# Attention, mixture-of-experts block on one core: row maxima turned into rows by VectorE instead of TensorE and ScalarE

## The reference

```
x:[8, 512, 512] fp32
x = x + layernorm(attention(layernorm(x)))      # 16 heads of 32, latent K/V/Q (128), rotary part shared by the heads
    c_kv, c_q = x @ W_DKV + b, x @ W_DQ + b
    k = [c_kv @ W_UK + b | (x @ W_KR + b) * pe],  q = [c_q @ W_UQ + b | (x @ W_QR + b) * pe],  v = c_kv @ W_UV + b
    attn = softmax(q . k / sqrt(32));  out = (attn @ v) @ W_O + b
x = x + layernorm(moe(layernorm(x)))            # 16 experts, top 2 of 16 in 2 of 4 groups, plus a shared expert (1024)
```

## Time and profile before

| | us |
|---|---|
| median of 3 runs | 1569.3 (1569.14 to 1573.41) |
| span of the profiled execution | 1566.3 |
| median less that span (what lies around it, and the spread of executions) | 3.0 |
| PE busy | 1498.5 (96%), 7006 instructions |
| DVE busy | 974.3 (62%), 1841 instructions |
| ACT busy | 783.3 (50%), 1415 instructions |
| POOL busy | 803.9 (51%), 812 instructions |
| POOL busy from 60 to 900 us | 633.75 of 840 |
| DVE busy from 60 to 900 us | 573.16 of 840 |

### The profile page before, as it was taken

How to read it: one execution, slowest core, us unless ns; L and a number is a source line. 1 busy time by engine, 2 the same in 40 slices (tenths; PEclk the granted TensorE clock), 3 DMA queues, 4 the chain that set the end, 5 groups by cost and what they waited for, 6 DMA issues and landing times.

```text
span 1566.3 us, 21725 instructions
## 1 busy us (share of the span) xinstructions
PE 1498.5 (96%) x7006; PEld 1018.5 (65%) x7006; DVE 974.3 (62%) x1841; ACT 783.3 (50%) x1415; POOL 803.9 (51%) x812
## 2 busy tenths in 40 slices
PE   5699999999999999999998999999999999999998
PEld 3355666656656666566564578778666666668886
DVE  3657676767676767767667454862333333349988
ACT  3265567566565675665647455422222222275554
POOL 1076787787776977877859630003222222143341
PEclk9699999999999999999999999999999999999999
DMA  5878669589495795884956421536987777697773
GB/s 130 138 100 135 101 109 213 74 173 172 82 179 111 121 211 74 181 156 85 222 97 129 135 79 67 198 121 196 311 235 219 210 215 221 195 349 241 232 241 125
DMA packets 163926, 257.75 MB, mean 165 GB/s; under 512 B 20100, under 2 KB 70404, under 8 KB 161764
## 3 DMA queue, kind: packets, MB, share of 16 engines
q1 hardware_dynamic: 144584, 204.98, 58.0%
q0 software_dynamic: 12784, 41.82, 9.4%
q10 hardware_dynamic: 6448, 9.57, 1.8%
HBM read 103.74 MB, written 58.46 MB: 104 GB/s over the span
## 4 chain that ended last, share of the span: by engine, by line
PE 71%; DMA 10%; DVE 7%; POOL 4%; issue 3%; ACT 2%; SPq 2%; DVEq 0%; POOLq 0%; ACTq 0%
PE bank L113 12%; PE bank L724 9%; PE bank L792 8%; PE bank L815 8%; PE bank L646 6%; PE bank L632 6%; DMA a<-a 6%; PE bank L662 6%; PE bank L651 6%; PE bank L746 5%; POOL a L1637 2%; PE bank L671 2%; DMA f<-f 1%; SPq L1875 1%; PE bank L804 1%
## 5 line engine op out<-in xcount | busy, mean ns | idle before, releaser
L1637 POOL TENSOR_TENSOR a<-a 128x512 f32<-128x512 f32 x384 | 499.5, 1329 | 100.2 <-ACT a L1443 54.5
L1443 ACT ACTIVATE a<-bank 128x512 f32<-128x512 f32 x512 | 296.4, 597 | 258.4 <-PE bank L651 218.4
L925 DVE TENSOR_REDUCE a<-bank 128x1 f32<-128x512 f32 x512 | 321.3, 680 | 80.2 <-PE bank L632 79.7
L113 PE MATMUL bank<-a 128*128 128x512 f32 (+1 forms) x864 | 238.9, 398 | 2.7 <-DVE s L877 1.6
L646 PE MATMUL bank<-a 128*128 128x512 f32 x512 | 217.3, 424 | 5.0 <-ACT a L1443 4.9
L651 PE MATMUL bank<-a 68*128 68x512 f32 x512 | 203.8, 398 | 0.4 <-ACT a L1433 0.2
L632 PE MATMUL bank<-a 128*128 128x512 f32 x512 | 181.0, 425 | 22.7 <-DMA a<-a 17.8
L113 PEld LDWEIGHTS bank<-a 128*128 128x128 f32 (+1 forms) x864 | 158.9, 186 | 49.1 <-issue 6.7
L1701 POOL DMA_INDIRECT f<-h_scratch,f x79 | 75.4, 954 | 224.5 <-DMA f<-f 203.6
L746 PE MATMUL bank<-c 128*128 128x512 f32 x768 | 178.2, 391 | 4.2 <-DVE c L983 2.1
L724 PE MATMUL bank<-c 128*128 128x512 f32 x768 | 177.4, 390 | 1.3 <-ACT c L1484 1.3
(11 more groups left out here) (190 smaller groups left out, 1766.9 us busy)
## 6 DMA issues: line engine op xcount, KB each, us to landing
a<-a SPq DMA_DIRECT2D x272, 256.0 KB, 9.7
f<-f SPq DMA_DIRECT2D x316, 64.0 KB, 3.9
yp_scratch<-f SPq DMA_DIRECT2D x79, 256.0 KB, 3.4
a<-in_L_attn_x SPq DMA_DIRECT2D x15, 1024.0 KB, 11.7
x_scratch<-a SPq DMA_DIRECT2D x8, 1024.0 KB, 4.6
h_scratch<-a SPq DMA_DIRECT2D x8, 1024.0 KB, 13.3
hT_scratch<-s SPq DMA_DIRECT2D x8, 1024.0 KB, 9.8
c<-hT_scratch SPq DMA_DIRECT2D x8, 1024.0 KB, 7.0
```

The costliest lines, as they stand in the source:

```text
L113: t = e.matmul(out, a[n], b[n], start=n == 0 and m == 0, stop=n == len(ah) - 1 and m == 2)
L925: e.tensor_reduce(K.mx[:, i, j:j + 1], K.MX[n % 3][:], AX.X, ALU.max).then_inc(Z.max, 1)
L1443: e.activation(K.pt[:, n % NP, :], K.SC[n % 2][:], ACT.Exp, scale=SCALE).then_inc(Z.exp, 1)
L1637: e.tensor_tensor(K.acc[:, j, :], a, K.pt[:, n % NP, :], ALU.add).then_inc(Z.acc, 1)
```

## The change

`rows` leaves the lists of PE and ScalarE and joins the list of VectorE at the same place in the order. `K.mx` becomes [128, 4, 32], set to zero once by POOL, so that each block i of maxima fills the first 4 of 32 columns. One block transpose of VectorE (32x32 blocks) turns the 128x128 of `K.mx` into `K.mt`, in which partition 32q + j holds the maxima of head j for queries 32q to 32q+31 of each block. Four multiplies by -1, one for each q, take 4 partitions and 4x32 elements each and write them to their columns of `K.QR[64:68]`. The `scores` matmuls wait for the new semaphore `max_rows_set`.

```diff
-FILLS = ("turn", "proj", "half", "rows", "v", "total", "project", "turn2", "route", "fold", "bias")
+FILLS = ("turn", "proj", "half", "v", "total", "project", "turn2", "route", "fold", "bias")
-    K.mx = tile([P, 4, 4])
+    K.mx = tile([P, 4, HD])
+    K.mt = tile([P, 4, HD])
 # tensor_program
-    def rows(u):
-        bank = begin("rows", u)
-        w.wait_ge(Z.max, 16 * (u + 1))
-        for i in range(4):
-            t = e.transpose(bank[0:4, i * P:(i + 1) * P], K.mx[:, i, :], K.ident[:])
-        t.then_inc(*end("rows", u))
     def scores(u, i, j):
...
-        drained("rows", u)
+        w.wait_ge(Z.rows, u + 1)
 # vector_program
     def top(u, j, i):
         n = 16 * u + 4 * j + i
         w.wait_ge(Z.top, n + 1)
+        w.wait_ge(Z.set, 3)
         if u:
-            m = K.fill["rows", u - 1]
-            w.wait_ge(Z.full[m % 2], m // 2 + 1)
+            w.wait_ge(Z.mT, u)
...
+    def rows(u):
+        w.wait_ge(Z.max, 16 * (u + 1))
+        if u >= 2:
+            w.wait_ge(Z.score, 16 * (u - 1))
+        if u:
+            w.wait_ge(Z.rows, u)
+        e.transpose(K.mt.rearrange("p i r -> p (i r)"), K.mx.rearrange("p i r -> p (i r)")).then_inc(Z.mT, 1)
+        w.wait_ge(Z.mT, u + 1)
+        tiles = K.QR[64:68, u % 2, :].rearrange("p (i q r) -> p i q r", q=4, r=HD)
+        for q in range(4):
+            t = e.tensor_scalar(tiles[:, :, q, :], K.mt[HD * q:HD * q + 4, :, :], -1.0, None, ALU.mult)
+        t.then_inc(Z.rows, 1)
 # scalar_program
-    def rows(u):
-        b = u // NG
-        bank = begin("rows", u)
-        if u >= 2:
-            w.wait_ge(Z.score, 16 * (u - 1))
-        e.mul(K.QR[64:68, u % 2, :], bank[0:4, :], -1.0).then_inc(*end("rows", u))
 # gpsimd_program
+    e.memset(K.mx, 0.0).then_inc(Z.set, 1)
```

More of the change, by code:

```diff
@@ L382, in __init__ @@
         self.x1, self.hi = make("x1_done"), make("kq_high")
-        self.top, self.max = make("top_full"), make("max_done")
+        self.top, self.max, self.rows, self.mT = make("top_full"), make("max_done"), make("max_rows_set"), make("max_turned")
         self.score, self.exp, self.acc, self.pv = make("score_full"), make("exp_done"), make("acc_done"), make("pv_done")
@@ L755, in totals @@
         e.matmul(K.TR[0][:], K.tri, flat, start=True, stop=True).then_inc(Z.totals, 1)
-        w.wait_ge(Z.set, 3)
+        w.wait_ge(Z.set, 4)
         e.matmul(K.TR[1][:], K.onesf, flat, start=True, stop=True).then_inc(Z.totals, 1)
@@ L817, in e_down @@
         t.then_inc(Z.ed, 1)
-    stages = {"turn": turn, "proj": proj, "v": v, "half": half, "bias": bias, "top": top, "rows": rows, "scores": scores,
+    stages = {"turn": turn, "proj": proj, "v": v, "half": half, "bias": bias, "top": top, "scores": scores,
               "values": values, "total": total, "project": project, "turn2": turn2, "route": route, "fold": fold, "up": up,
@@ L1342, in finish @@
         e.tensor_tensor(K.x1[:, z, :], K.x1[:, z, :], K.sh[:, z, :], ALU.add).then_inc(Z.co, 1)
-    stages = {"stat": stat, "aggr": aggr, "sel": sel, "split w": split_w, "turn": turn, "low": low, "proj": proj, "half": half, "bias": bias, "top": top, "invert": invert,
+    stages = {"stat": stat, "aggr": aggr, "sel": sel, "split w": split_w, "turn": turn, "low": low, "proj": proj, "half": half, "bias": bias, "top": top, "rows": rows, "invert": invert,
               "project": project, "fold": fold, "split h": split_h, "split up": split_up, "split down": split_down, "up": up,
@@ L1601, in finish @@
                      scale=K.crw[:, z, 4, 0:1]).then_inc(Z.cn, 1)
-    stages = {"split w": split_w, "round": round_, "scale": scale, "turn": turn, "proj": proj, "v": v, "half": half, "rows": rows, "scores": scores, "keep": keep,
+    stages = {"split w": split_w, "round": round_, "scale": scale, "turn": turn, "proj": proj, "v": v, "half": half, "scores": scores, "keep": keep,
               "turn2": turn2, "route": route, "split h": split_h, "split up": split_up, "round up": round_up,
```

## The result

The changed kernel takes 1661.6 us (median of 5, 1660.5 to 1665.1), the one before 1569.3 on the same chip: ratio 1.0586 [1.057, 1.0602], slower. Predicted were 1650 and a range to 1672. The profiled execution of after has a span of 1660.3 us, 94.0 above.

The account below looks back on a forecast made before the run. PE bounds the kernel (71% of the chain that ended last). Six third/fourth pairs +64, seven first/second pairs -6, units 1 to 3 +14, unit 30 +3, unit 31 +7: +82 us, said as 1650; range 1572 to 1672, likeliest case 1605 to 1672.

Parts of the forecast that it names:

- What goes: On PE, four transposes and the longer step behind them go: 0.44 us a unit, 14 us if all on the path.
- The chain alone: Block transpose, semaphore and four multiplies on DVE with nothing holding them up: 1.15 us, the low bound.
- The chain beside POOL: DVE multiplies and POOL adds take turns of 1.35 us: rest of the running add + 4.2 us; chance 0.68.
- Third unit: Third unit of a batch (as unit 10): chain ends 5.7 us after 320.0, PE waits about 3.9 us; +5.3 us.
- Fourth unit: Fourth unit of a batch (as unit 11): chain 5.3 us, PE +3.9, 0.5 given back at the stack's DMA: +3.4 us.
- First and second: First and second units of a batch: a 3.4 us chain fits DVE's idle time; -0.9 us for both, -6 over seven pairs.
- The clock: PE at 0.50 after long pauses loses about 2 us each: hidden by DVE in third units, +2.0 us in fourth.
- Units 1 to 3: Same three kinds of place without the statistics, 4 to 5 us each with the clock: +14 us.
- Unit 30: Near the end: +3 us, its LayerNorm statistics waiting for a residual add anyway.
- Unit 31: Rows stand behind `split up` and `low(29)` on DVE; PE up to 8.6 us late, part covered by POOL: +7 us.
- What would show it: If right: multiplies' mean 1.3 to 1.5 us, longest over 1.4, PE idle 3 to 4 us in third and fourth units.
- One wait, then all four run: Rival: multiplies take no turns, chain is the rest of the running add + 0.6 us; 1579 us, chance 0.12.

Follow-up runs that it names:

- The version with early reductions: Changed kernel with one-element reductions for the four multiplies and the rows moved earlier in the order: 1574.2 us, ratio 0.9974 to the kernel before.
- the reductions (278 ns at the same place): Changed kernel with each of the four multiplies replaced by a one-element maximum, same place and order: 1582.9 us, ratio 1.0037 to the kernel before.
- the kernel before with multiplies: Kernel before plus an unused block transpose and four multiplies on DVE: 1629.2 us, ratio 1.0322; its twin with reductions instead: 1580.5 us, 1.0018.
- the 230 trials: Two small separate kernels (54 and 176 trials), DVE multiplies asked at varied offsets beside POOL adds: first multiply 1.34 us at most, later ones 1186 to 1210 ns.

## Why the prediction was right, and where not

- *What goes.* Right: 0.44 us a unit of PE. The version with early reductions shows it in two of four kinds of unit (second and fourth); in the other two PE gets it and loses it again to ScalarE and the stack's transfers.
- *The chain alone.* Block transpose 0.303 us for 0.31. The four moves at 219 ns for 0.2. At unit 0, with POOL quiet, 1.26 in all for 1.15.
- *The chain beside POOL.* The choice for exclusion and for turns was right, and it made the sign and most of the size. The choice rested on L903 and L979; the reductions (278 ns at the same place) and the kernel before with multiplies (1.0322 against 1.0018) show that it is this exclusion and not the load on DVE. A turn costs 1.21 us, not 1.35: the short DVE part runs where one POOL add gives way to the next, and POOL loses nothing. The rows had a sign of it: L903 ended 0.28 us after the add, though its own length is 0.42, and the multiplies of 0.22 end 0.09 after it.
- *Third unit.* The sum was right (+5.3 predicted, +5.1 to +5.2 measured), its working was not. r was 1.46 and came out as 1.47, but there are no turns behind it: four more adds pass first, and the chain is 7.1 us from the end of L878, not 5.7, so PE waits 4.9 at L645 instead of 3.9. What I had added for the line behind (the maxima 5.2 late) is not paid a second time: PE has stood in front of L645 for as long, and its wait for maxima stays at 5.2 us in total. Where PE doesn't wait for the rows the line is a cost of its own, as the kernel before with multiplies shows. So the +5.3 came out by luck, from two errors of about a microsecond and of opposite sign.
- *Fourth unit.* Chain 5.0 for 5.3, wait 3.8 for 3.9. The stack's DMA wait is gone, as said: of nine waits one is left.
- *First and second.* Here the sum failed: -6 over seven pairs predicted, +7 measured, and the forecast of +82 is 12 short of the span's +94. They do fit, though barely: 4.2 us for 3.4 in the second, since three multiplies and not two meet an add. But a loss lies in them that I had put elsewhere, the next point. In the last batch (28 and 29, +2.8 and +1.3) the first unit has four turns and PE waits 1.9.
- *The clock.* The step was there, too small and in the wrong place: 2.0 us a batch for the fourth unit's pause, nothing for the third's, which DVE was to hide. It shows in the unit behind each pause. The fourth unit is 5.7 us later (mean) with 3.8 of waiting, and had 0.4 to gain: 2.3 for the clock behind the third unit's pause, 2.5 when PE's other short waits are set against those of before. The first unit is 0.7 later with no wait, had 0.4 to gain, and is spared another 0.4 of the stack's DMA wait (that was the 0.5 given back): 1.6 behind the fourth's. These sizes are those of the lower level: at 0.50 from 349.3 to 355.7 PE does half of 6.4 us of work, 3.2 us less, and by this reckoning the clock makes unit 11 3.2 later; behind unit 14's pause PE works 3.3 us at 0.50, and unit 15 is 1.7 later. That is why the fourth units differ, from +4.2 to +6.5. Third and fourth units together, with the clock, were put at 64 and are 65; the 2.0 a batch is about what the third unit's pause alone cost. What was missing is the fourth's 1.6, and it shows in the first units. The prediction named this as what would make the time high ("if the third unit's clock loss is not hidden").
- *Units 1 to 3*: +14 predicted, 11.2 measured from unit 0 to unit 3. *Unit 30*: +3, measured +1.2. *Unit 31*: +7, measured +9.1: less of PE's delay was covered by POOL than I let. Behind it 1.4 more. All terms as measured: 10.1 + 65.3 + 7.0 + 1.2 + 9.1 + 1.4 = 94.1, the first of them from the start.
- *What would show it.* The multiplies' mean of 1.04 us is under the 1.3 to 1.5 that I named, since behind the long wait three of four go through at 0.22, and in the first units nearly all. The longest and the places of PE's waits told the mechanism where the mean did not.
- *The rivals.* "One wait, then all four run" gave 1579 from r + 0.6. It is what the third units look like, only that the wait is for all of POOL's line and not for one add. I had not thought of that case.

The Trainium skill, "SBUF — State Buffer", section "SBUF: two separate sides", has the lock held for the whole instruction. The fourth units and the 230 trials agree, 1.21 us a multiply. The 6.2 and 9.7 us of the third units, through five and eight instructions, are not in it, and here the measurement goes further than the page.

## What to carry to other kernels

Beside a busy POOL a small DVE instruction in SBUF is cheap only if it isn't one that excludes POOL: ask for each added instruction which kind it is and what POOL has in line just then, not what share of DVE is busy. Where the wait counts, in these runs a form that does not exclude does the same move (a reduction over one element: 278 ns always, against 219 alone and 1040 here), and a few places earlier in the order turn the rest into a small gain (0.26%). Where one delay reaches an engine by two ways, count the later, not the sum, and look for the clock's loss in the unit behind the pause.

## What I had not expected of the hardware

- A multiply of 4x128 fp32 that asks during a POOL add mostly gets in at its end (1.21 us a turn, POOL's pace of 1.22 unchanged), but in one place of this kernel it is kept out until POOL pauses: 6.2 us through five adds, 9.7 through eight, and the same instruction in another batch 1.1 to 1.3.
- When a multiply starts just before an add instead, the add pays: in the trials an add that met a running multiply lasted up to 1.33 us and moved the next by 0.07, no more.
- ScalarE's move of 4x128 takes 0.307 us against 0.22 on DVE and 0.278 as a reduction.
- Pauses of 3.8 and 4.9 us each put PE at 0.50 for the 3.1 to 6.4 us of work behind them, and behind the third units' pauses about half of that time, 1.7 to 3.2 us, was lost.
